# A one-core Flamingo block kernel: tokens split 14 and 18 tiles with five scatters or gathers under way, and the second attention's normalisations on ScalarE with a bias from GpSimd

## The reference

```python
x = x + tanh(g_xattn[0]) * attention_8_wide_heads(layernorm(x), ctx)          # 32 query heads, 8 kv heads
x = x + tanh(g_ffn[0])   * mixture(layernorm(x))                              # 64 experts, top 8, plus a shared expert
x = x + tanh(g_xattn[1]) * (attention_16_wide_heads(layernorm(x), ctx) @ Wc.T + bc)
x = x + tanh(g_ffn[1])   * fp8_mlp(layernorm(x))                              # per-tensor abs-max scale over all tokens
```

## Time and profile before

| | |
|---|---|
| median of 3 runs | 1281.42 us (1279.56 to 1288.40) |
| profiled execution | 1274.8 us, of which the profiled span is 1273.0 us |
| busy over the span | DVE 83%, PE 69%, POOL 56%, ACT 55% |
| routing | 197.9 to 350.4 us |
| wait for the first half's scatters | 350.4 to 393.9 us |
| groups 0 to 47, 48 to 95 | 393.9 to 607.9 us, 607.9 to 828.9 us |
| second attention and its lead in and out | 828.9 to 1103 us |
| FP8 feed-forward | 1103 to 1273 us |

### The profile page before, as it was taken

How to read it: one execution, slowest core, us unless ns; L and a number is a source line. 1 busy time by engine, 2 the same in 40 slices (tenths; PEclk the granted TensorE clock), 3 DMA queues, 4 the chain that set the end, 5 groups by cost and what they waited for, 6 DMA issues and landing times.

```text
span 1273.0 us, 31296 instructions
## 1 busy us (share of the span) xinstructions
PE 883.2 (69%) x9384; PEld 626.0 (49%) x9394; DVE 1050.5 (83%) x2644; ACT 702.0 (55%) x1370; POOL 718.4 (56%) x800
## 2 busy tenths in 40 slices
PE   5789984465405888786777777756687778576665
PEld 3445552333204777675666666634455555322332
DVE  6789997988804889997589999966998888598998
ACT  4679994455303656655455555533555555515763
POOL 3557773777777565555347776456878882280000
PEclk9899995555557999999799999968899999888887
DMA  5977771222226999997899999985223330000011
GB/s 132 260 234 230 225 220 63 88 96 101 103 98 220 330 308 326 325 323 251 255 311 326 324 308 326 293 201 105 72 83 93 93 87 13 1 0 1 34 46 53
DMA packets 198114, 221.48 MB, mean 174 GB/s; under 512 B 44957, under 2 KB 176862, under 8 KB 197726
## 3 DMA queue, kind: packets, MB, share of 16 engines
q1 hardware_dynamic: 173406, 152.70, 39.0%
q0 software_dynamic: 24576, 67.14, 16.5%
HBM read 114.64 MB, written 105.12 MB: 173 GB/s over the span
## 4 chain that ended last, share of the span: by engine, by line
DMA 26%; DVE 23%; POOL 19%; issue 15%; PE 7%; ACT 5%; SPq 4%; DVEq 0%; POOLq 0%; ACTq 0%
DMA xs<-V 12%; POOL xs L757 7%; DMA V<-ys,idx 4%; DVE arena L1557 4%; POOL region L734 3%; DMA arena<-in_wpairs 3%; POOL arena L734 3%; DVE HM L1525 3%; DMA xs<-arena,V 2%; DMA arena<-ys,idx 2%; POOL V L734 2%; DVE x L1442 2%; DVE arena L1555 2%; ACT arena L804 2%; PE bank L1618 1%
## 5 line engine op out<-in xcount | busy, mean ns | idle before, releaser
L757 POOL DMA_INDIRECT xs<-V x192 | 191.1, 996 | 117.4 <-DMA xs<-V 59.8
L1734 PE MATMUL bank<-arena,region 128*128 128x128 f16 x2496 | 227.8, 230 | 0.4 <-ACT arena L919 0.3
L1808 PE MATMUL bank<-arena 128*128 128x128 f16 x1536 | 152.9, 224 | 96.5 <-DMA arena<-xs 95.9
L1734 PEld LDWEIGHTS bank<-arena,region 128*128 (+1 forms) x2496 | 174.3, 103 | 6.9 <-issue 0.8
L1808 PEld LDWEIGHTS bank<-arena 128*128 128x128 f16 x1536 | 102.8, 100 | 106.8 <-DMA arena<-xs 106.7
L919 ACT COPY arena<-bank 128x1024 f16<-128x1024 f16 x96 | 96.8, 1008 | 92.3 <-PE bank L1808 92.0
L934 ACT CAST arena<-arena 64x512 f16<-64x512 f32 x96 | 59.3, 618 | 140.0 <-DVE arena L1476 138.3
L804 ACT ACTIVATE arena<-bank 128x512 f32<-128x512 f32 x192 | 108.1, 604 | 47.8 <-PE bank L1618 47.4
L1066 DVE TENSOR_REDUCE arena<-bank 128x8 f32<-128x512 f32 x192 | 122.6, 679 | 10.6 <-PE bank L1604 8.8
L1460 DVE COPY arena<-bank 128x1024 f16<-128x1024 f16 x96 | 65.3, 681 | 78.8 <-PE bank L1808 78.0
L1837 PE MATMUL bank<-region,arena 128*128 x384 | 91.4, 278 | 51.4 <-DVE arena L1490 38.6
(11 more groups left out here) (229 smaller groups left out, 2253.0 us busy)
## 6 DMA issues: line engine op xcount, KB each, us to landing
arena<-xs SPq DMA_DIRECT2D x384, 128.0 KB
ys<-arena SPq DMA_DIRECT2D x96, 512.0 KB
xs<-idx SPq DMA_DIRECT2D x52, 256.0 KB, 3.1
arena<-in_wpairs SPq DMA_DIRECT2D x32, 256.0 KB, 2.9
arena<-in_wpairs SPq DMA_DIRECT2D x64, 128.0 KB, 3.2
out<-arena SPq DMA_DIRECT2D x16, 256.0 KB, 2.2
xs<-idx SPq DMA_DIRECT2D x8, 384.0 KB, 3.7
xs<-V POOLq DMA_INDIRECT x192
```

Of the source, the lines that this page charges most:

```text
L757: pool.indirect_dma_start(xs[half_of(t)], bass.IndirectOffsetOnAxis(ap=at_row[:, t, n % 8:n % 8 + 1], axis=0), ROW[t % NROW], None).then_i ...
L1734: mm = pe.matmul(o, lhs(a, w, k), rhs(a, w, k), start=(n == 0), stop=(n == 3 * KT - 1))
L1808: mm = pe.transpose(tpm[q // 2][:, q % 2, m, :], RAW[g % 2][:, q, m * P:(m + 1) * P], rcv("ident"))
```

## The change

Five things change together.

- `HALF` is (14, 18). The first half has 176 expert tiles (44 groups), the second 208 (52 groups), still 96 groups. The first half has 112 scatters, gathers and sums, the second 144. The space of an expert in `xs` grows from 17 to 19 tiles of rows (`RS`), in DRAM. Sums of the first half now start at group 52 and go over 44 groups.
- `NSENT` and `NGOT` are 5, on shared semaphores.
- `NROW`, the ring of rows that wait for their scatter, has 25 buffers for 23. Two tiles' weights (`W8X`) are kept in another place, since 18 do not fit in `W8L`.
- SP's loads of the second attention's first keys come at group NG + 4 and DVE's bias rows at NG + 9, which are groups 48 and 53 as before. SP also waits there for the keys' maxima (`key8`), which are done by group 42.
- In the second attention the two normalisations of a step leave DVE (`norm`, `query`) for ACT (`normed`, an Identity activation with scale rs and bias -mean * rs). They stand behind the Q2 copy in ACT's order. POOL makes that bias with two more small tensor_tensors in `deviations` (times -1, times rs), and waits there for ACT's older normalisations. DVE's wait on `rs2` moves behind the absolute maximum, which now waits for ACT (`LND["out"]`). ACT's steps are written out with no loop.

The core of the diff:

```diff
 NHALF = 2
-HALF = (16, 16)
+HALF = (14, 18)
 HT = HALF[0]
+HX = max(HALF)
 FROM = (0, HT, NT)
...
 TILES = tuple(-(-(8 * n + E - 1) // GT) * GT for n in HALF)
-TMAX = TILES[0]
+TMAX = max(TILES)
 NG = TILES[0] // GT
 NGG = sum(TILES) // GT
-NROW = 23
+NROW = 25
 NSLOT = 3
 LNB = 8
-RS = HT * P + P
+RS = HX * P + P
 XROWS = E * RS + P
...
 AHEAD = 3
-NSENT = 3
-NGOT = 4
+NSENT = 5
+NGOT = NSENT
 BK = 97
...
     d_xr = [sem(f"d_xr{i}") for i in range(4)]
-    got = [sem(f"got{i}") for i in range(NGOT)]
     il_zero = sem("il_zero")
     sent = [sem(f"sent{i}") for i in range(NSENT)]
+    got = sent
 
...
         return 16 * len(range(i, 8 * tiles_sent, NSENT))
+
+    def got_count(i, gathered):
+
+        return sent_count(i, NT) + 16 * len(range(i, gathered, NGOT))
 
...
             for i in range(NGOT):
-                eng.wait_ge(got[i], 16 * len(range(i, 8 * (tile + 1), NGOT)))
+                eng.wait_ge(got[i], got_count(i, 8 * (tile + 1)))
 
...
                     store(g - 1)
-                if g == NG:
+                if g == NG + 4:
+                    sp.wait_ge(M["key8"], NT // 2)
                     sp.wait_ge(kd_zero, 2)
...
             pool.memset(ZERO, 0.0).then_inc(half_set, 1)
-            pool.wait_ge(half_set, 3)
+            pool.memset(minus[:, :], -1.0).then_inc(half_set, 1)
+            pool.wait_ge(half_set, 4)
 
...
                 pool.tensor_tensor(ve[:, at, :], mv[:, at, 1:2], epsilon[:, :].unsqueeze(1).to_broadcast([P, k, 1]), ALU.add).then_inc(ve2, 1)
-                pool.wait_ge(ve2, n)
-                pool.tensor_tensor(rs[:, at, :], ve[:, at, :], neghalf[:, :].unsqueeze(1).to_broadcast([P, k, 1]), ALU.pow).then_inc(rs2, 1)
+                if inside(t + 2):
+                    pool.wait_ge(LNA["out"], STAT_BASE[2] + t + 3)
+                if inside(t - 5):
+                    pool.wait_ge(LND["out"], t - 4)
+                pool.tensor_tensor(away[:, at, :], mv[:, at, 0:1], minus[:, :].unsqueeze(1).to_broadcast([P, k, 1]), ALU.mult).then_inc(ve2, 1)
+                pool.wait_ge(ve2, 3 * n - 2)
+                pool.tensor_tensor(rs[:, at, :], ve[:, at, :], neghalf[:, :].unsqueeze(1).to_broadcast([P, k, 1]), ALU.pow).then_inc(ve2, 1)
+                pool.wait_ge(ve2, 3 * n)
+                pool.tensor_tensor(away[:, at, :], away[:, at, :], rs[:, at, :], ALU.mult).then_inc(rs2, 1)
 
...
                 if n >= NGOT:
-                    pool.wait_ge(got[n % NGOT], 16 * (n // NGOT))
+                    pool.wait_ge(got[n % NGOT], got_count(n % NGOT, n))
                 if k == 0 and t >= NSLOT:
...
                     act.activation(EX[4 * j + n], bank[4 + n], ACT.Exp, scale=d ** -0.5).then_inc(a["ex_ready"], 1)
+
+                def normed(dst, src, n, l):
+                    act.activation(dst, src, ACT.Identity, bias=away[:, n, :], scale=rs[:, n, :]).then_inc(l["out"], 1)
 
...
                         act.copy(Q2[1 - j], bank[0].rearrange("p (g s) -> p g s", g=G)).then_inc(a["q2_ready"], 1)
+                    if layer == 1 and t + 4 >= 1 and inside(t + 3):
+                        act.wait_ge(rs2, t + 4)
+                        normed(XG[(q + 3) % NXG].rearrange("p g (n w) -> p g n w", n=npair)[:, :, :, 0:2 * d].rearrange("p g n (k d) -> p g n k d", d=d),
+                               tile_x(t + 3).rearrange("p (n k g d) -> p g n k d", n=npair, g=G, d=d), 1 - j, LNA)
+                    if layer == 1 and inside(t - 4):
+                        act.wait_ge(rs2, t + 4)
+                        if past(t, 6):
+                            act.wait_ge(F["tp_ready"], t - 5)
+                            act.wait_ge(F["am_done"], t - 5)
+                        normed(XD[j], tile_x(t - 4), 2 + j, LND)
                     if layer == 1 and inside(t - 2):
...
 
-                sweep(act, step, LAST[layer], 12 if layer else 4)
+                if layer == 0:
+                    sweep(act, step, LAST[layer])
+                else:
+                    for t in range(-3, LAST[layer] + 1):
+                        step(t, t % NKD)
 
...
                     sums_within(t, 3)
-                    if t + 4 >= 1 and (inside(t + 3) or inside(t - 4)):
-                        dve.wait_ge(rs2, t + 4)
-                    if inside(t - 4):
-
-                        if past(t, 6):
-                            dve.wait_ge(F["tp_ready"], t - 5)
-                        norm(t - 4, 2 + j, 3, XD[j], tile_x(t - 4))
-                    if inside(t + 3):
-                        query(t + 3, 1 - j, (q + 3) % NXG)
                     if inside(t - 4):
...
                     sums_within(t, 4)
+                    if t + 4 >= 1 and (inside(t + 3) or inside(t - 4)):
+                        dve.wait_ge(rs2, t + 4)
                     if inside(t - 3):
...
 
-                if g == NG + 5:
+                if g == NG + 9:
                     bias_rows()
...
                     dve.wait_ge(M["wt"], 1)
-                    dve.tensor_copy(W8L, W8[:, HT:NT, :]).then_inc(M["w8"], 1)
+                    dve.tensor_copy(W8L, W8[:, HT:HT + 16, :]).then_inc(M["w8"], 1)
+                    dve.tensor_copy(W8X, W8[:, HT + 16:NT, :]).then_inc(M["w8"], 1)
 
...
                 t, n = m // ADDS, m % ADDS
-                w = (W8[:, t, :] if t < HT else W8L[:, t - HT, :])
+                w = (W8[:, t, :] if t < HT else W8L[:, t - HT, :] if t < HT + 16 else W8X[:, t - HT - 16, :])
                 rows = SLOTS[half_of(t)][t % NSLOT].rearrange("p (k h) -> p k h", k=8)
...
                     if t == HT:
-                        dve.wait_ge(M["w8"], 1)
+                        dve.wait_ge(M["w8"], 2)
                 else:
...
                 dve.scalar_tensor_tensor(tile_x(t), rows[:, n, :], w[:, n:n + 1], tile_x(t), ALU.mult, ALU.add).then_inc(M["cb"], 1)

```

More of the change, by code:

```diff
@@ L125, in tile_columns @@
     at, out = 0, {}
-    for name, width in (("tix", TMAX), ("t128", TMAX), ("thr", HT), ("ebase", 1)):
+    for name, width in (("tix", TMAX), ("t128", TMAX), ("thr", HX), ("ebase", 1)):
         out[name] = (at, at + width)
@@ L141, in tile_table @@
     put("t128", np.arange(TMAX)[None, :] * P + P)
-    put("thr", np.arange(HT)[None, :] * P)
+    put("thr", np.arange(HX)[None, :] * P)
     put("ebase", np.minimum(np.arange(P), E - 1)[:, None] * RS + P)
@@ L229, in flamingo_block @@
     rs = sb("rs", [P, 4, 1])
-    arena_bytes = 51 * 1024
+    away = sb("away", [P, 4, 1])
+    minus = sb("minus", [P, 1])
+    arena_bytes = 52864
     arena = sb("arena", [P, arena_bytes // 4])
@@ L286, in flamingo_block @@
     spare = arena[:, last_at - XW // 2:last_at].bitcast(F16)
-    ROW = [kept16[:, XW * n:XW * (n + 1)] for n in range(9)] + [carve([XW], F16) for _ in range(NROW - 16)]
-    ROW += [kept16[:, XW * n:XW * (n + 1)] for n in range(9, 15)] + [spare]
+    ROW = [kept16[:, XW * n:XW * (n + 1)] for n in range(7)] + [carve([XW], F16) for _ in range(NROW - 18)]
+    ROW += [kept16[:, XW * n:XW * (n + 1)] for n in range(7, 15)] + [spare]
+    ROW += [arena[:, last_at - XW // 2 - NHALF * E - XW // 2 * n:last_at - XW // 2 - NHALF * E - XW // 2 * (n - 1)].bitcast(F16) for n in (2, 1)]
     at_row = kept.bitcast(I32)[:, 15 * XW // 2:15 * XW // 2 + NT * 8].rearrange("p (t k) -> p t k", k=8)
@@ L311, in flamingo_block @@
     ZERO = idx[:, :, :].rearrange("p t k -> p (t k)").bitcast(F16)
-    assert used[0] <= off_at, used[0]
+    assert used[0] <= off_at - XW, used[0]
     used[0] = after_table
@@ L321, in flamingo_block @@
     YS = [carve([GT, H]) for _ in range(2)]
-    P8, K8A, W8 = (carve([NT, 8]) for _ in range(3))
+    P8, K8A = (carve([NT, 8]) for _ in range(2))
     K8B = P8
-    SUW = carve([NT])
-    EB, KA, KB = (carve([2, E]) for _ in range(3))
+    SUW = rsr[:, :, 0]
+    W8X = ver[:, 0:8 * (HALF[1] - 16), :].rearrange("p (t k) a -> p t (k a)", k=8)
+    EB = carve([2, E])
+    W8 = arena[:, used[0]:used[0] + NT * 8].rearrange("p (t k) -> p t k", k=8)
+    KA, KB = (carve([2, E]) for _ in range(2))
     bias_part, one16 = EB[0:1].rearrange("p a e -> p (a e)").bitcast(BF16), FS[:, 14:15].bitcast(BF16)[:, 0:1]
-    assert used[0] <= off_at, used[0]
+    assert used[0] <= off_at - XW, used[0]
     xs = [nc.dram_tensor(f"xs{h}", (XROWS, XW), F16, kind="Internal").ap() for h in range(NHALF)]
@@ L346, in flamingo_block @@
     hb = region[:, 24576:].bitcast(BF16)
-    W8L = fr[:, 24832:24832 + HALF[1] * 8].rearrange("p (t k) -> p t k", k=8)
+    W8L = fr[:, 24832:24960].rearrange("p (t k) -> p t k", k=8)
     SLOTS = [[last_kb] + [kept[:, n * 8 * H:(n + 1) * 8 * H] for n in range(2)],
```

2 lines of the change are left out of this document (1 added, 1 removed).

## The result

The kernel after takes 1297.36 us (median of 9 runs, 1290.54 to 1302.30), against 1281.42 us before (9 runs): a ratio of 1.0123, with a 95% interval of 1.0094 to 1.0151. It is slower by 1.2%. So the two traces lie 27.5 us apart where the medians lie 16 apart: their difference has to be read by stage, not by sum.

What follows compares the result with a forecast made beforehand. First-half scatters bound the experts' start, nearly full DMA engines and DVE the experts, POOL the second attention. -21.9, +3.0, -7.7, +35 and +7 make +15.4 us: 1290 profiled, 1296 forecast from the median; range 1262 to 1312.

Steps and rivals of the forecast that it cites:

- the experts' term: Whole expert stage, from its start to group 95: ends 26.6 us earlier, 18.9 by group 48 and 7.7 after.
- Start of the experts, -21.9: First half's scatters: two tiles less to scatter, so group 0 starts 21.9 us earlier, at 372.0.
- Groups 0 to 48, +3.0: Scatters at 1.35 us, groups at 4.6, stall about gone: group 48 at 589, 18.9 us earlier, 3.0 of the gain lost.
- the rival of room in them: Groups 0 to 48: DMA engines have room, groups hold 4.27 us, experts gain 38; 1285 us, chance 0.15.
- my slow-scatter rival: Second half's scatters stay at 1.73 us, group 48 comes 26 us late; 1341 us, chance 0.06.
- Groups 48 to 95, -7.7: Fewer sums per group, 2.55 instead of 3.2: groups take 4.33 us, 7.7 us less, bounds 0 and 13.
- neither theory: Second attention: loop theory has the ring through PE, ACT and DVE set the pace; POOL theory, the forecast, has POOL.
- Second attention, POOL, +35: Steps 1 to 24: more gathers +20.4 us, two bias operations +14.4; POOL paces at 9.1 us a step, bounds 27 and 45.
- The loop through ACT, nothing in steps 1 to 24: Second attention: DVE's maximum waits for ACT, a loop of 8.4 us, shorter than POOL's 9.1, so adding nothing.
- Tail and lead-in, +7: Second attention's ends: loop on the path in the tail, +6 us, bounds 0 and 10; lead-in +1.
- The loop as limit: Second attention: POOL hides its additions in gaps and the 8.4 us loop is the limit; 1280 us, chance 0.13.
- DVE as the limit: Second attention: DVE is the limit and ACT's normalisation early enough, 0.41 us less a step; 1245 us, chance 0.11.

Runs made afterwards that it cites:

- Split and five: Kernel after with both normalisations back on DVE and no bias operations on POOL, keeping halves 14 and 18 and five under way: 1269.74 us, ratio 0.993.
- five alone: Kernel after with normalisations back on DVE, no POOL bias and halves of 16, five scatters or gathers under way: 1267.55 us, ratio 0.9911 to before.
- the slower chip: Chip of the first four experiments, on which the kernel before takes 1601.99 us.
- split with three: Kernel after with normalisations back on DVE, no POOL bias, halves 14 and 18, but three under way: 1309.87 us, ratio 1.0258 to before.
- the normalisations alone: Kernel before with only the second attention's normalisations moved to ACT and their bias made on POOL: 1325.99 us, ratio 1.0367.
- XD comes ahead of Q2: Kernel after with ACT's normalisation of XD placed ahead of the Q2 copy: 1283.64 us, ratio 1.0079 to before.
- XD on DVE: Kernel after with XD's normalisation back on DVE, the query's on ACT, POOL's bias operations kept: 1274.51 us, ratio 0.9957 to before.

## Why the prediction was right, and where it was right by accident

1296 was forecast and 1297.36 measured, slower as the largest chance had it. But part of this is luck. By the stages of the two traces the change costs 27.5 us where the sum had +15.4: -11.7 up to group 95 (forecast -26.6), -0.9 in the lead-in, +33.8 in steps 1 to 24, +7.2 in the tail, -1.0 behind it. The medians are only 15.9 us apart, since the traced run of before lies 6.6 us under its median, for which the forecast allowed, and that of after 4.9 us above its own. So the experts' term missed by 14.9 us, and the two traced runs stand 11.6 us further apart than the medians; in which stage that lies can't be told. That the total was met so closely is no merit of the experts' term. And within the second attention two errors cancel.

- **Start of the experts, -21.9.** Right. Group 0 came 17.6 us earlier in the profile, with a first scatter that was itself 2.8 us later (215.51 for 212.71), so -20.4 relative to it. Split and five against five alone: -19.2.
- **Groups 0 to 48, +3.0.** Right, term by term. A scatter takes 1.34 us (1.35 forecast), the last one starts at 560.3 (561 forecast for its landing), the stall is gone, group 48 starts at 591.9 (589 forecast), and the time from group 0 to group 48 has grown by 1.7 us. The step that I could not read from a row, what five under way make of a scatter, was rightly taken from the gather. My 4.6 us for a group beside scatters came out as 194.6 / 43 = 4.53; my 4.0 for a group without them is borne out on the slower chip, 3.9 to 4.2. But the DMA engines were not full at 324 GB/s: they moved 329, and 339 to 340 in the kernels with five and DVE's normalisations, so the rival of room in them was partly true: in split and five a group takes 190.1 / 43 = 4.42. That five are needed for the split is shown by split with three: group 48 at 623.1, 40 us behind split with five, by the mechanism of my slow-scatter rival (634 forecast). Up to group 43 its groups take 185.7 / 43 = 4.32 us against 4.42 with five; without the split it is 183.6 us for 43 groups with three (before) and 189.4 with five. In that direction the traces agree with the rule on turns between the queues that I cited from the Trainium skill ("DMA: Bandwidth & Descriptors", section "SWDGE vs HWDGE vs iDMA"), by 0.10 to 0.13 us a group; they don't show the turns themselves.
- **Groups 48 to 95, -7.7.** Failed. After has +4.3 here, split with five +1.4. Groups 48 to 52, which I had left as they were, take 25.1 us for 22.4. Groups 52 to 60 take 40.6 for 34.9; the sums now begin at group 52 and not at 56. The rest runs at 155.2 / 35 = 4.43 us, 4.55 before. So the lighter load came, and the first twelve groups lost more than it gave. That the earlier sums are the reason is likely but not shown: with five alone, where the sums begin at group 56, groups 52 to 60 take 37.2 us, and with the normalisations alone even 38.7, as in split with five. In that last kernel, where no line of this stage is changed, groups 48 to 95 took 227.8 us, with the DMA engines moving 292 GB/s for 308. Why is open; it belongs to neither theory.
- **Second attention, POOL, +35.** The number was right, 217.4 for 183.7 = +33.7, and the reason wrong. This is the step that failed. Gathers alone raise a plain step by 0.72 us (7.32 to 8.04), near my 0.85, and the four rounding steps by 3.0 together: +17.4 for +20.4. That part holds, and POOL is full in the kernel that has it alone. But the two bias operations of a step, for which I took 0.6 us, cost 0.04 while the loop is slower (8.44 to 8.40), 0.29 where XD comes ahead of Q2 (8.40 to 8.11), and 0.20 with XD on DVE (8.24 against 8.04 in split with five), though they are busy for 0.55. The rest lies in the base: my 7.65 a step was the mean of 7.32 in 20 steps and 9.3 in four, so POOL's wall in a plain step is at 8.24 and not at 9.1. With XD on DVE, where POOL paces, steps 1 to 24 take 204.9 us, so POOL alone costs +21 and my term had 14 too much. The loop, which I had put at nothing, brought the other 12.5 us. That the two are alike is chance.
- **The loop through ACT, nothing in steps 1 to 24.** It was my next wall at 8.4 us, and its size was right: 8.28 in the kernel with the normalisations alone, where POOL has 24 us to spare. The activation takes 592 ns, not the 0.53 us that I worked out. I had not put the weight rounding into it. It stands in the ring, between the statistics and L1103, so that the four steps together grew by 8.4 us over split with five, and by 10.4 where the normalisations came alone. Part of that, at PE's lower granted clock, no term of mine had either. Over steps 1 to 24 the parts alone cost +17.4 (split) and +29.7 (normalisations), together +33.8: in each step the later wall counts, not the sum.
- **Tail and lead-in, +7.** Right: the tail is 7.2 us longer, the lead-in 0.9 shorter (1 longer was forecast). Alone the normalisations cost 9.8 us there.
- **The rivals.** The loop as limit was the right mechanism with the chance 0.13. It gave 1280, for it had the loop's 8.4 us in every step and nothing more in the rounding ones, and -26.6 from the experts, of which -11.7 came. With 20 steps of 8.4 us, the four rounding steps at their 48.7, and the experts' -11.7 it would have been 1274.8 - 11.7 + (168 + 48.7 - 183.7) + 7 = 1303, near the profiled 1302.3. This uses measured steps, so it only shows that the terms close. DVE as the limit is refuted by 52.9 us of its idle time before one instruction.

The page "ScalarE: Activation LUTs" of the Trainium skill, section "What ACT_TABLE_LOAD costs", gave 586 ns for that activation, an estimate; by the row of L827, 592 ns, the trace agrees. Its section "Table sets" has identity in every set, and here too the trace agrees: the kernel after has three table loads of 1283 ns each, as many as before, none between the exponentials.

## What to carry to other kernels

Work that leaves a nearly full engine for an idle one can lengthen a ring: look for an instruction of the relieved engine that now waits for a result made behind that engine's own last product, and add up the ring with the longest piece of work that stands in any step of it. Read the pace of a stage over equal steps, not as a mean over steps with different work, before adding costs to it. Where an engine waits is to be read step by step too: most of POOL's waits stood in four steps of 24. A right total is no proof of a reason; the parts run alone did not add up, and that showed two walls of nearly equal height.
